# A 16-image attention and conditional-convolution kernel on one core: key tiles in turns of four, and VectorE's two-operand work moved to GpSimd and ScalarE

## The reference

```
layer 0 (attention):
  xn = group_norm(x, 32 groups) * gn_w + gn_b
  q, k, v = split(qkv_w @ xn + qkv_b)            # 4 heads of 64, 1024 positions
  p = softmax(q^T k / 8)                         # per head 1024 x 1024
  x = x + proj_w @ (p v) + proj_b
layer 1 (conditional convolution):
  rw = sigmoid(mean(x) @ router_w^T + router_b)  # 8 gates per image
  W1, W2, W3 = sum over experts e of rw[e] * w1[e], w2[e], w3[e]
  out = relu(bn1(conv1x1(x, W1)))                # 256 -> 64
  out = relu(bn2(conv3x3(out, W2)))              # 64 -> 64
  x = relu(bn3(conv1x1(out, W3)) + x)            # 64 -> 256
```

## Time and profile before

| | |
|---|---|
| runs shown | 2118.03, 2100.87, 2117.54 us, median 2117.54 |
| profiled execution | 2096.82 us, span 2095.0 us from first to last instruction |
| TensorE busy | 1960.1 us |
| VectorE busy | 1440.0 us |
| GpSimd busy | 1118.7 us |
| ScalarE busy | 1045.7 us |
| mean granted TensorE clock | 0.984 |
| moved by DMA | 119.35 MB, mean 57 GB/s |

### The profile page before, as it was taken

One profiled execution on the slowest core, in us unless ns is written; L12 is line 12 of the kernel. 1 busy time (PEld: TensorE's weight loads), 2 busy tenths in 40 slices (PEclk: granted clock), 3 DMA queues, 4 the chain that ended last, 5 costly groups with the idle time before them and its releaser, 6 DMA issues.

```text
span 2095.0 us, 26308 instructions
## 1 busy us (share of the span) xinstructions
PE 1960.1 (94%) x8072; PEld 1061.8 (51%) x8072; DVE 1440.0 (69%) x1638; ACT 1045.7 (50%) x1346; POOL 1118.7 (53%) x533
## 2 busy tenths in 40 slices
PE   4999999999999999999999989999899999999994
PEld 3555555545555455555555545455554555545431
DVE  5658768486784957758586785857858587685743
ACT  3555545454555444555454555454554455554441
POOL 3665555464555545555464564645555555554660
PEclk9999999999999999999999999999999999999997
DMA  3112131121313012130121312113130121301201
GB/s 137 42 26 82 36 101 26 44 74 31 101 31 96 20 36 91 32 105 20 41 81 31 101 30 65 47 36 96 31 101 18 38 87 34 101 24 43 56 27 61
DMA packets 65694, 119.35 MB, mean 57 GB/s; under 512 B 20480, under 2 KB 21248, under 8 KB 65536
## 3 DMA queue, kind: packets, MB, share of 16 engines
q1 hardware_dynamic: 65664, 118.97, 19.4%
HBM read 54.68 MB, written 17.04 MB: 34 GB/s over the span
## 4 chain that ended last, share of the span: by engine, by line
PE 79%; DVE 12%; issue 5%; DMA 2%; ACT 2%; DVEq 0%; SPq 0%; POOL 0%; ACTq 0%
PE PV L590 19%; PE SB L461 12%; PE S L574 11%; PE MS L555 10%; PE S L577 9%; PE SB L498 5%; PE SB L532 4%; DVE mx L763 4%; DVE mix L854 3%; PE SB L492 3%; PE SB L540 3%; DVE rden L841 2%; PE SB L519 1%; DVE o L836 1%; DVE x_lo L755 1%
## 5 line engine op out<-in xcount | busy, mean ns | idle before, releaser
L447 POOL TENSOR_TENSOR psum_p<-psum_p,prob 128x1024 f32<-128x1024 f32 x384 | 931.1, 2425 | 596.4 <-ACT prob L654 589.0
L763 DVE TENSOR_REDUCE mx<-MS 128x1 f32<-128x1024 f32 x500 | 609.9, 1220 | 416.1 <-PE MS L555 413.9
L654 ACT ACTIVATE prob<-S 128x1024 f32<-128x1024 f32 x512 | 523.7, 1024 | 405.1 <-PE S L577 398.6
L590 PE MATMUL PV<-prob,V 128*64 128x512 f32 x2048 | 506.9, 617 | 0.0
L574 PE MATMUL S<-Q,K 128*128 128x512 f32 x1024 | 455.1, 444 | 2.5 <-DVE mx L910 2.5
L577 PE MATMUL S<-Q,K 128*128 128x512 f32 x1024 | 406.1, 397 | 0.3 <-DMA Q<-mrow 0.3
L555 PE MATMUL MS<-K,Q 128*128 128x512 f32 x1000 | 327.8, 409 | 73.3 <-DVE mx L763 73.2
L574 PEld LDWEIGHTS S<-Q,K 128*128 128x128 f32 x1024 | 194.3, 190 | 264.9 <-issue 231.4
L447 POOL TENSOR_TENSOR psum_p<-prob 128x1024 f32<-128x1024 f32 x64 | 151.7, 2370 | 311.3 <-ACT prob L654 311.3
L590 PEld LDWEIGHTS PV<-prob,V 128*64 128x64 f32 x2048 | 125.5, 137 | 266.4 <-issue 240.5
L555 PEld LDWEIGHTS MS<-K,Q 128*128 128x128 f32 x1000 | 176.5, 188 | 162.5 <-DVE mx L763 131.2
(11 more groups left out here) (126 smaller groups left out, 1879.8 us busy)
## 6 DMA issues: line engine op xcount, KB each, us to landing
xin<-in_x_dram SPq DMA_DIRECT2D x16, 1024.0 KB, 8.7
K<-K SPq DMA_DIRECT2D x128, 128.0 KB, 2.2
Q<-Q SPq DMA_DIRECT2D x128, 128.0 KB, 2.3
rz<-z_dram SPq DMA_DIRECT2D x128, 128.0 KB, 2.9
x<-in_x_dram SPq DMA_DIRECT2D x16, 1024.0 KB, 6.2
out_dram<-y SPq DMA_DIRECT2D x64, 256.0 KB, 2.1
V<-v_next SPq DMA_DIRECT2D x16, 512.0 KB, 6.5
hpad<-hpad SPq DMA_DIRECT2D x16, 289.0 KB, 3.1
```

The lines of the kernel that those rows point to most:

```text
L447: nc.gpsimd.tensor_tensor(acc, first_in, prob[:, s % PBUF, :, :], ALU.add).then_inc(add_done, 1)
L590: last = nc.tensor.matmul(PV[own(a), :], V[:, b // NH, kt, a * D:a * D + D], prob[:, s % PBUF, a, :], start=(kt == 0), stop=(kt == KT - 1))
L654: nc.scalar.activation(prob[:, s % PBUF, :, :], S[:, s % 2, :, :], ACT.Exp, scale=D ** -0.5).then_inc(exp_done, 1)
L763: nc.vector.reduce_max(mx[:, b % 2, m:m + 1], MS[:, :, :], AX.XY).then_inc(max_read, 1)
```

## The change

- PV and the sums behind it run for four key tiles at once (BATCH = 4): on TensorE a step n is scores, fill, the jobs of PLACES[n], and after each fourth step come four PVs and the HALVES jobs. prob has eight places; fills run 13 steps ahead.
- Each engine has a table by step: PLACES (bank jobs), WORK (VectorE), ACT_WORK, POOL_WORK and LOADS (SP).
- z and two of the four conv3 jobs use half of MS, or the free part of it, in place of SB; the next fill waits for their reader.
- z is four matmuls of 32 columns by 256 pixels, each in a quarter of the array's columns; its result is read as 256 columns. The very last block's denominators are inverted where they lie, 512 columns, with no trip through DRAM.
- conv3 uses the 64 rows of the array that hold its half of the pixels, and mix itself, where it used all 128 with a zero-padded copy, mix3.
- q and k: ScalarE makes the rounded part straight from the bank with the bias, and VectorE the remainder from the bank by one operation with the bias (scalar_tensor_tensor); qk_raw is gone, and the bank is free only after VectorE's read.
- The expert sum: ScalarE multiplies an expert by its gate in place (`product`), GpSimd adds (`mix_add`). Only two experts lie in SBUF; SP loads each again from DRAM when the sum before has freed its place (`load_expert`). In the last image the other six are loaded into tiles no longer used, and VectorE's chain stays.
- GpSimd also takes split_x, the product of normalise_o, the small group-norm operations (`deviations`) and the addition in gates. The router's averages are read by a broadcast operand of four matmuls, without pool2 and poolb.
- The image is loaded in quarters (four DMAs of 256 KB), for both xin and x2; hpad's upper half is written by two more activations and not by a DMA.

```diff
-PBUF = 4
+PBUF = 8
...
+BATCH = 4
+TURNS = STEPS // BATCH
+PLACES = {0: [("proj", -1, 0)], 1: [("qk", 0, 6)], 3: [("row", 0, 1)], 4: [("gna", 1, 0), ("proj", -1, 1)], 5: [("gnb", 1, 0)],
+          6: [("qk", 0, 7)], 8: [("proj", -1, 2)], 9: [("proj", -1, 3)], 10: [("router", -1, 0)], 11: [("row", 0, 2)],
+          12: [("qk", 1, 0)], 15: [("qk", 1, 1)], 16: [("qk", 1, 2)], 18: [("v", 1, 0)], 19: [("row", 0, 3), ("v", 1, 1)],
+          21: [("qk", 1, 3)], 24: [("v", 1, 2)], 26: [("v", 1, 3)], 27: [("row", 1, 0)], 28: [("qk", 1, 4)], 30: [("qk", 1, 5)]}
+HALVES = {1: [("z", 0, 0)], 3: [("z", 0, 1)], 4: [("conv1", -1, 0)], 5: [("conv2a", -1, 0), ("conv2", -1, 0), ("z", 0, 2)],
+          6: [("conv3", -1, 0), ("conv3", -1, 1)], 7: [("conv3", -1, 2), ("conv3", -1, 3), ("z", 0, 3)]}
+PROLOGUE = [("gna", 0, 0), ("gnb", 0, 0)] + [("qk", 0, f) for f in range(4)] + [("v", 0, f) for f in range(4)] + [("qk", 0, 4), ("qk", 0, 5), ("bias", 0, 0)]
+EPILOGUE = ([("proj", 0, f) for f in range(4)] + [("router", 0, 0), ("conv1", 0, 0),
             ("conv2a", 0, 0), ("conv2", 0, 0)] + [("conv3", 0, f) for f in range(4)])
-AHEAD = 4
+AHEAD = 5
...
+WORK = {0: [("proj", -1, 0), ("stats", 1, 0)], 1: [("qk", 0, 6)], 3: [("stats", 1, 1), ("row", 0, 1), ("gna", 1, 0)],
+        4: [("recip", -1, 3), ("proj", -1, 1), ("gnb", 1, 0)], 7: [("qk", 0, 7)], 8: [("proj", -1, 2)],
+        9: [("recip", 0, 0), ("proj", -1, 3)], 10: [("router", -1, 0), ("gates", -1, 0)], 11: [("row", 0, 2)], 13: [("qk", 1, 0)],
+        15: [("qk", 1, 1)], 17: [("qk", 1, 2)], 18: [("recip", 0, 1), ("row", 0, 3)], 23: [("qk", 1, 3)],
+        27: [("recip", 0, 2), ("row", 1, 0), ("conv3", -1, 0), ("conv3", -1, 1)], 29: [("qk", 1, 4)],
+        31: [("qk", 1, 5), ("conv3", -1, 2), ("conv3", -1, 3)]}
+ACT_WORK = {6: [("normal", 1, 0)], 9: [("normal", 1, 1)], 11: [("product", -1, 0), ("product", -1, 1)], 12: [("product", -1, 2)],
+            15: [("product", -1, 3), ("product", -1, 4)], 16: [("product", -1, 5), ("product", -1, 6)], 18: [("product", -1, 7)]}
+POOL_WORK = {4: [("deviations", 1, 0)], 5: [("affine", 1, 0)], 6: [("norm", -1, 3)],
+             10: [("split", 1, 0), ("split", 1, 1), ("gates", -1, 0)], 11: [("mix", -1, 1)], 13: [("mix", -1, 2)],
+             15: [("mix", -1, 3), ("mix", -1, 4)], 17: [("mix", -1, 5)],
+             19: [("mix", -1, 6), ("mix", -1, 7), ("norm", 0, 0), ("norm", 0, 1)], 30: [("norm", 0, 2)]}
+LOADS = {1: [("v1", 0, 0)], 14: [("xin", 2, 0)], 15: [("xin", 2, 1)], 16: [("xin", 2, 2)], 28: [("xin", 2, 3)]}
...
-        ex = sb("ex", [P, E, MIX])
+        ex = sb("ex", [P, 2, MIX])
...
+            def load_expert(i, e):
+                wait(sp, mix_chain, (E - 1) * i + (max(1, e - 2) if e >= 2 else e - 1))
+                sp.dma_start(ex[:, e % 2, :], experts[:, e, :]).then_inc(ex_loaded[e % 2], 16)
...
+                        for e in ((0, 1) if (kind, f) == ("mix", 1) else (f,) if kind == "mix" else ()):
+                            load_expert(i + di + (e + 2) // E, (e + 2) % E)
+                    if n % BATCH == BATCH - 1:
+                        for kind, di, f in jobs_of(HALVES, n // BATCH, first, last):
+                            if kind == "z" and f < BLOCKS - 1:
+                                move_z(i + di, f)
+                            if kind == "conv3":
+                                store(i + di, f)
+                                load_x2(i, f)
...
+            def mix_add(i, e):
+                pool.wait_ge(product_ready, E * i + e + 1)
+                if e == 1:
+                    wait(pool, filled["conv3"], 4 * i)
+                    others = ex[:, 0, :]
+                else:
+                    pool.wait_ge(mix_chain, (E - 1) * i + e - 1)
+                    others = mix[:, :]
+                nc.gpsimd.tensor_tensor(mix[:, :], others, ex[:, e % 2, :], ALU.add).then_inc(mix_chain, 1)
...
+                    for kind, di, f in jobs_of(POOL_WORK, s, first, last):
+                        if kind == "gates":
+                            gates(i + di)
+                        if kind == "deviations":
+                            deviations(i + di)
+                        if kind == "affine":
+                            affine(i + di)
+                        if kind == "split":
+                            split_x(i + di, f)
+                        if kind == "norm":
+                            normalise_o(i + di, f)
+                        if kind == "mix":
+                            mix_add(i + di, f)
...
+                        for g in range(4):
+                            last = nc.tensor.matmul(MS[32 * g:32 * g + 32, 0, 0:HALF // 2], ones[:, 0:32],
+                                                    psum_p[:, f % 2, g // 2, g % 2 * (HALF // 2):g % 2 * (HALF // 2) + HALF // 2],
+                                                    start=True, stop=True)
...
-                    last = nc.tensor.matmul(bank, mix3[:, hf, oc * P:oc * P + P], h2[:, :], start=True, stop=True)
+                    wait(pe, max_read, fills)
+                    last = nc.tensor.matmul(bank, mix[own(hf), M1 + M2 + oc * P:M1 + M2 + oc * P + P], h2[own(hf), :], start=True, stop=True)
...
+                for n in range(STEPS):
+                    if n + 2 < STEPS:
+                        scores(i, n + 2)
+                    elif not last:
+                        scores(i + 1, n + 2 - STEPS)
+                    at = fill_at(i, n, last)
+                    if at:
+                        max_fill(*at, lent)
+                        lent = []
+                        fills = 32 * at[0] + 8 * at[1] + at[2] + 1
+                    for kind, di, f in jobs_of(PLACES, n, first, last):
+                        job(kind, i + di, f, held)
                         held = [(kind, i + di, f)]
+                    if n % BATCH == BATCH - 1:
+                        for s in range(n + 1 - BATCH, n + 1):
+                            pv(i, s)
+                        for kind, di, f in jobs_of(HALVES, n // BATCH, first, last):
+                            if borrows(kind, f):
+                                job(kind, i + di, f, [], MS[:, 1, :], fills=fills)
+                                lent = lent + [(kind, i + di, f)]
+                            else:
+                                job(kind, i + di, f, [] if kind == "conv2" else held, fills=fills)
+                                held = [(kind, i + di, f)]
...
+                        nc.scalar.activation(dst[own(a), 2 * p + a, px(hf)], bank[own(a), :], ACT.Identity,
+                                             bias=vec[own(a), col:col + 1]).then_inc(qk_hi, 1)
...
+            def product(i, e):
+                act.wait_ge(ex_loaded[e % 2], 16 * (E // 2) * i + 16 * (e // 2) + 16)
+                if e == 0:
+                    act.wait_ge(rw_chain, i + 1)
+                nc.scalar.activation(ex[:, e % 2, :], ex[:, e % 2, :], ACT.Copy, scale=rw[:, e:e + 1]).then_inc(product_ready, 1)
...
-                        last = nc.vector.tensor_tensor(dst, qk_raw[own(a), f % 2, :], hi[own(a), h, px(hf)].bitcast(F32), ALU.subtract)
+                        last = nc.vector.scalar_tensor_tensor(out=dst, in0=bank[own(a), :], scalar=vec[own(a), col:col + 1],
+                                                              in1=hi[own(a), h, px(hf)].bitcast(F32), op0=ALU.add, op1=ALU.subtract)
...
-                nc.vector.tensor_scalar(rden[:, :], rexp[:, :], 1.0, None, ALU.add).then_inc(rw_chain, 1)
-                dve.wait_ge(rw_chain, 2 * i + 1)
+                dve.wait_ge(rw_ready, i + 1)
+                wait(dve, product_ready, E * i)
                 nc.vector.reciprocal(rw[:, :], rden[:, :]).then_inc(rw_chain, 1)
```

More of the change, by code:

```diff
@@ L384, in _ @@
+                    for kind, di, f in LOADS.get(n, []):
+                        if kind == "xin" and more:
+                            load_xin(i + di, f)
+                        if kind == "v1":
+                            load_v1(i + di)
+                if first:
+                    for f in range(4):
+                        load_x2(i, f)
+            for f in range(4):
+                load_xin(0, f)
             sp.dma_start(vec[:, :], vecs).then_inc(norm_loaded, 16)
@@ L463, in split_mm, with job @@
                 return last
[L465 removed]
+            def job(kind, i, f, before, bank=SB[:, :], at_end=False, fills=0):
                 for k, bi, bf in before:
```

400 lines of the change are left out of this document (197 added, 203 removed).

## The result

The kernel before ran at a median of 2114.99 us (7 runs beside the changed one, 2100.87 to 2118.03), the changed kernel at **2087.64 us** (7 runs, 2081.78 to 2090.64). The ratio is **0.9883, 95% interval 0.9855 to 0.9911**: 1.2% faster. Its profiled execution took 2085.19 us, span 2083.4; that of before 2096.82 and 2095.0. The two profiled executions are thus only 11.6 us apart, the medians 27. The traces explain the 11.6; what experiment 13 says of the rest stands there.

A forecast was written before the change was run, and what follows sets the result against it. TensorE was taken to bound the kernel, with 8.4 us of waits per image. Against the profiled execution, +3.5+1.5-14x1.4-12.7-10.7 = -38 gave 2059 us; the carried 20.7 us gap to the median made 2080, range 1990 to 2140.

The forecast's parts named there:

- Fewer visits, -2.8: TensorE's PV for four tiles at once: eight fewer switches to column halves and back, 0.35 us each, -2.8 us per image.
- Quarters and row halves overlap: On TensorE, z's four column-quarter matmuls and conv3's two row-half matmuls run in parallel: -1.7 us per image each.
- rival 2: Array shapes do not overlap, or the visit's price scales with PV count: 2134 us, or 2125; chance 0.15.
- Waits return at bare steps, 12.4: TensorE waits again at steps with only scores and fill, and at other listed places: together 12.4 us per image.
- Rival 1: TensorE's waits are smaller than walked, about half fall away: -6.2 us per image, 1993 us; chance 0.18.
- Inner images, 14 x -1.4 = -19.6: Fourteen inner images take 125.1 us (112.7 work plus 12.4 waits) instead of 126.5, each 1.4 us less.
- VectorE's lateness goes: With most two-operand work gone, VectorE no longer collides with GpSimd and its late reads, largest wait 1.73 us, vanish.
- GpSimd 94 of 125 us, no slack: GpSimd is busy 94 of 125 us per image; its seventh expert sum just meets TensorE at conv1, nothing charged.
- The ring costs nothing to 4.3 us: Reloading experts into two SBUF places costs only slack while a load lands within 4.3 us; 4.0 assumed.
- rival 3: Expert reloads take 7 us to land and hold exponentials, z and conv1: +98 us, 2178 us; chance 0.17.
- Last image -12.7: Last image's section, 115.2 us before, is bounded by GpSimd: 36.5 to n=11 plus 66 is 102.5 us.
- Behind it -10.7: Work behind the last image: -7.4 from inverting denominators in place, -1.6 from clock, -1.7 from conv3 pair.

The follow-up runs named there:

- experiment 13: Kernel before, its VectorE expert sums, splits of x and normalisations of o replaced by maxima over one SBUF operand (results left out): 2035.3 us, ratio 0.9673.
- experiment 1: Changed kernel with PV in turns of two key tiles instead of four: 2078.8 us, ratio 0.9869 to the kernel before.
- experiment 2: Changed kernel with denominators as two matmuls of 64 columns over 512 pixels instead of four of 32 over 256: 2094.3 us, ratio 0.9943.
- experiment 10: Changed kernel run once more, unaltered: 2086.8 us, ratio 0.9911 to the kernel before.
- experiment 9: Changed kernel with the last image section's expert products and sums on 8 columns instead of 768: 2081.0 us, ratio 0.9877.
- experiments 5 and 12: 5: changed kernel, last denominators read before conv3's activations, 2079.1 us. 12: the same plus PV in turns of two, q 3 subtracted one step earlier, 2053.2 us.

## Why the prediction came out as it did

Predicted 2080 us, measured 2087.6, inside the range, 1.2% faster where faster was the likeliest. **Part of that is luck.** The sum made 2059 for the profiled execution, which took 2085.2; the 20.7 us carried from profiled execution to median hid this, since the changed kernel's median stands only 2.5 above its profiled execution.

- *Fewer visits, -2.8.* Nearly right: 2.4 by experiment 1. The changes between array shapes cost the 0.1 us assumed (0.52 from a record to the next of another shape, as at 1047.17 and 1047.69, against 0.42 or 0.43 within one).
- *Quarters and row halves overlap.* Right: eight records of the denominators and two pairs of conv3 show it; rival 2 is out. Quarters are worth 0.8 us of the 1.7, by experiment 2.
- *Waits return at bare steps, 12.4.* Right as a sum: images without slow stretch take about 125.6 us, forecast 125.1. The view lists 9.4 us of waits and leaves 116.2, where the forecast had 12.4 and 112.7; in the kernel before it lists 5.0 where the same count gave 8.4, so both times some 3 us stand in no list. By place: n=0 about 1.2 (forecast 1.5), n=3 1.8 (1.8), n=4 to 6 1.2 (1.0), bare steps 0.64 to 0.74 each (0.6 to 0.7), n=18 1.75 (1.55). Rival 1 is out.
- *Inner images, 14 x -1.4 = -19.6.* Measured -8.0. The walk knew one clock. Four images with a slow stretch, 1.6 us longer each, are 6.5 of the 12 us; the other 0.4 or so per image is the walk's own. I had a 1.8 us wait at n=3 in it and did not ask what the clock does behind it, though the earlier trace rows showed a clock of 0.99. Nor was 126.5 the undisturbed image: it is a mix of 125.9 (slow stretch) and 127.4 (a second collision at the full clock).
- *VectorE's lateness goes.* Right, and larger than written: 3.9 us per image in the kernel before (experiment 13). The Trainium skill (GPSIMD Engine Reference, Specifications) says that GpSimd shares its SBUF interfaces with VectorE, and that instructions of VectorE with two SBUF inputs contend for them; by that rule, the runs agree (1.02 against 2.80 us, and 0.95 for a maximum over one input).
- *GpSimd 94 of 125 us, no slack.* It was 91 (1273.96/14), and conv1 does not wait in inner images. *The ring costs nothing to 4.3 us.* Right, 3.5 and no effect; rival 3 is out.
- *Last image -12.7: wrong, +5.3* (+2.8 in experiment 10). The step that failed is 36.5+66 = 102.5. The 36.5 is counted from TensorE's step n=0 (the same walk has the copy of q 6 issued 9.7 us in; it is 8.2 us behind the scores of n=0 and 17.3 behind the first exponential), but the section it was set against begins at the first exponential, 9.1 us earlier. From n=0 to n=11 it was 39.6, and behind n=11 72.9 instead of 66, for I let GpSimd run without a gap. With that, half of the miss is a wrong start of the count; that GpSimd alone bounds the rest is wrong too, by experiment 9.
- *Behind it -10.7:* -9.9. The reciprocal of 512 columns in place took 3.35 us instead of 2.3:

```profile
2043.34 0.60 ACT L823 ACTIVATE rz<-MS 128x512 f32<-128x512 f32 x1 [1.84 <-PE MS L612]
...
2044.03 3.35 DVE L980 RECIPROCAL rz<-rz 128x512 f32<-128x512 f32 x1 [3.30 <-ACT rz L823]
```

- *Prologue +3.5 and first image +1.5:* +1.3 and -0.3, both over-priced.

**Where the gain went.** Taking two-operand work off VectorE alone is worth about 68 us (experiment 13, which leaves the work out rather than moves it); the whole change brought 27. Turns of four are not what took the rest: in turns of two (experiment 1) the kernel is 9 us faster, with intervals that overlap, and its inner images still list 101.7 us of waits, where experiment 13 lists 36.6. The largest are for MS while the denominators use it (19.9) and for the bank SB until VectorE has read q or k (13.9 and 12.2). That these new holders of MS and SB take the gain is a reading of these lists; the orders of experiments 5 and 12, which shorten one such wait each, gain 0.8 and 1.1 us per image in turns of two. The kernel before with only its splits and sums moved to GpSimd was not tried; these runs point to it.

## What to carry to other kernels

Before re-batching to save a fixed price per visit, look at what the visit hides: here 2.4 us of switches were the cover for 2.1 us of single-buffer turnaround. Price an operation by its duration in the loop and idle (3.00 against 1.21 us for the same split) and ask first whether only that can be changed. When a forecast walks through waits, mark those over a microsecond, since the lower clock may follow, and look image by image at which way that moves the time: 1.6 us longer here, 1.5 us shorter in the kernel before. And when a walk gives an absolute time, check that it starts at the event where the measured stretch starts.
